# Weighing the values for two 64-query blocks at a time, left and right column halves of the array in turn

## The reference

```python
# layer 0: 16 heads of 8, values shared by 4 heads; window of 64 keys back
logits = masked_attn * gene_fitness[..., None] + (1.0 - mask) * -10000000000.0
attn_w = softmax(logits, axis=-1)
out = einsum('bhts,bhsd->bhtd', attn_w, v_full)        # then out @ w_o + b_o
# layer 1: 16 heads of 8, windows of 64 that overlap by half, blended
attn = softmax(einsum('bqd,bkd->bqk', qw, kw), axis=-1)
wo = einsum('bqk,bkd->bqd', attn, vw)                  # windows blended, then @ wproj + bproj
```

## Time and profile before

| | us |
|---|---|
| median of 2 runs | 1242.99 |
| lowest and highest run | 1239.91, 1246.08 |
| span of the profiled execution | 1243.5 |
| PE busy, weight loads busy | 793.3 (64%), 631.3 (51%) |
| DVE, ACT, POOL busy | 548.2, 305.2, 116.8 |

### The profile page before, as it was taken

How to read it: one execution, slowest core, us unless ns; L and a number is a source line. 1 busy time by engine, 2 the same in 40 slices (tenths; PEclk the granted TensorE clock), 3 DMA queues, 4 the chain that set the end, 5 groups by cost and what they waited for, 6 DMA issues and landing times.

```text
span 1243.5 us, 17236 instructions
## 1 busy us (share of the span) xinstructions
PE 793.3 (64%) x6608; PEld 631.3 (51%) x6608; DVE 548.2 (44%) x1386; ACT 305.2 (25%) x584; POOL 116.8 (9%) x139
## 2 busy tenths in 40 slices
PE   0623589658865886589074468756966795678055
PEld 0623367527652765277063347644855584467033
DVE  0261730573057205720266454557354656455232
ACT  0202431243124322431110123212213221231023
POOL 4140000000000000000522200000000000000500
PEclk9999765676567656755555675567557655855577
DMA  6004000400040004000100320041013002200101
GB/s 186 0 28 117 27 6 1 109 26 4 0 110 25 4 0 110 25 4 0 34 1 15 100 56 6 1 110 30 0 44 92 4 0 63 72 4 0 34 1 34
DMA packets 69458, 46.05 MB, mean 37 GB/s; under 512 B 13368, under 2 KB 60986, under 8 KB 69434
## 3 DMA queue, kind: packets, MB, share of 16 engines
q1 hardware_dynamic: 66970, 39.97, 11.6%
q0 software_dynamic: 2464, 5.77, 1.5%
HBM read 37.85 MB, written 7.86 MB: 37 GB/s over the span
## 4 chain that ended last, share of the span: by engine, by line
PE 48%; DVE 24%; ACT 8%; issue 6%; POOL 6%; SPq 4%; DMA 4%; POOLq 0%; DVEq 0%; ACTq 0%; another core or an unknown queue 0%
PE ps_turn L799 18%; PE ps_score L702 4%; DVE gm L570 3%; DVE tsum L568 3%; DVE gm L574 3%; PE ps_turn L689 3%; DMA b2r<-in_L_b2e 3%; PE ps_score L774 3%; PE ps_score L710 3%; POOL sorted_x L1049 2%; POOL moe L1058 2%; PE ps_score L778 2%; DVE v L515 2%; ACT qT L854 2%; PE ps_proj L809 2%
## 5 line engine op out<-in xcount | busy, mean ns | idle before, releaser
L799 PE MATMUL ps_turn<-v,pT 128*64 128x9 f32 (+1 forms) x2048 | 220.6, 276 | 6.7 <-ACT pT L890 4.4
L799 PEld LDWEIGHTS ps_turn<-v,pT 128*64 128x64 f32 x2048 | 214.4, 221 | 12.0 <-issue 8.1
L702 PE MATMUL ps_score<-xgT,w 128*128 128x128 f32 x384 | 88.4, 402 | 39.2 <-ACT xgT L833 39.2
L702 PEld LDWEIGHTS ps_score<-xgT,w 128*128 128x128 f32 x384 | 75.6, 293 | 54.6 <-ACT xgT L833 54.6
L456 POOL TENSOR_TENSOR ys<-ys,b2r 128x128 f32<-128x128 f32 x48 | 24.7, 515 | 823.0 <-ACT ys L844 823.0
L890 ACT ACTIVATE pT<-ps_score 128x1024 f32<-128x1024 f32 x64 | 64.7, 1023 | 136.9 <-PE ps_score L778 136.8
L699 PE MATMUL ps_score<-ident,xg 128*128 128x128 f32 x48 | 19.7, 411 | 96.6 <-DMA b2r<-in_L_b2e 64.7
L836 ACT ACTIVATE hT<-ps_score,b1s 128x128 f32<-128x128 f32 x192 | 54.7, 368 | 87.6 <-PE ps_score L702 87.6
L635 DVE RECIPROCAL wtot<-ps_turn 128x16 f32<-128x16 f32 x16 | 4.1, 257 | 161.9 <-PE ps_turn L799 161.9
L710 PE MATMUL ps_score<-w,hT 128*128 128x128 f32 x384 | 72.6, 364 | 0.0
L710 PEld LDWEIGHTS ps_score<-w,hT 128*128 128x128 f32 x384 | 71.5, 284 | 0.0
(11 more groups left out here) (215 smaller groups left out, 1331.6 us busy)
## 6 DMA issues: line engine op xcount, KB each, us to landing
w<-in_L_w1e SPq DMA_DIRECT2D x48, 256.0 KB, 2.8
w<-in_L_w2e SPq DMA_DIRECT2D x48, 256.0 KB, 3.0
xg<-sorted_x SPq DMA_DIRECT2D x48, 64.0 KB, 1.9
b2r<-in_L_b2e SPq DMA_DIRECT2D x48, 64.0 KB, 3.2
sorted_y<-ys SPq DMA_DIRECT2D x48, 64.0 KB, 1.6
sorted_x<-moe POOLq DMA_DIRECT2D x2, 768.0 KB, 7.3
out<-x SPq DMA_DIRECT2D x4, 256.0 KB, 2.3
b1s<-in_L_b1e SPq DMA_DIRECT2D x48, 2.0 KB, 2.6
```

The lines of the kernel that those rows point to most:

```text
L702: ins = te.matmul(ps_score[:, k, c * P:(c + 1) * P], w1[:, j % WS, c * P:(c + 1) * P], xgT[:, k, :], start=True, stop=True)
L799: ins = te.matmul(o, w_, r, start=True, stop=True)
```

## The change

`weigh` takes a tile of two blocks instead of one block; inside the loop over heads it issues the matmul of the even block and then that of the odd one, so that consecutive loads go to the left and the right 64 columns in turn. `s_pv` is raised once per tile. `probs` are issued two at a time, ahead of the `weigh` of the tile before. `pT` has four buffers; `th` is now the last two of them. ACT's order of work is the same; exp of block u waits for `weigh` of tile u // 2 - 2 from u = 4 on.

```diff
--- before.py
+++ after.py
@@ -139,8 +139,8 @@
         qT = sb("qT", [P, 8, T], BF16)
         kT = sb("kT", [P, 8, 64 + T + 64], BF16)
         v = sb("v", [P, NU, H * 36])
-        th = sb("th", [P, 2, 1024])
-        pT = sb("pT", [P, 2, 1024])
+        pT = sb("pT", [P, 4, 1024])
+        th = pT[:, 2:4, :]
         gm = sb("gm", [P, NT, H * 4])
         tsum = sb("tsum", [P, NT, H])
         inv = sb("inv", [P, NT, H])
@@ -629,7 +629,7 @@
                         keep_odd(2 * NT + t, qT[:, :, t * P:(t + 1) * P])
 
                     for t in range(NT):
-                        dv.wait_ge(s_pv, 2 * t + 2)
+                        dv.wait_ge(s_pv, t + 1)
                         if L == 0:
                             o = ps_turn[:, 0, 0:H * 9].rearrange("p (h e) -> p h e", e=9)
                             st(nc.vector.reciprocal(wtot[:, :], o[:, :, 8]))
@@ -781,22 +781,23 @@
                                                 start=m is None, stop=True, skip_group_check=True)
                         ins.then_inc(s_st, 1)
 
-                    def weigh(u):
-
-                        te.wait_ge(s_p, u + 1)
-                        t, blk = u // 2, u % 2
-                        if blk == 0 and t >= 1:
+                    def weigh(t):
+
+                        te.wait_ge(s_p, 2 * t + 2)
+                        if t >= 1:
                             te.wait_ge((s_hd if L == 0 else s_osb), t)
                         for h in range(H):
                             hf, par, j = h // 8, h // 4 % 2, h % 4
-                            w_ = pT[:, u % 2, par * 512 + (4 * hf + j) * 64:par * 512 + (4 * hf + j) * 64 + 64]
-                            if L == 0:
-                                o = ps_turn[64 * blk:64 * blk + 64, 0, 9 * h:9 * h + 9]
-                                r = v[:, u, 9 * (h // 4):9 * (h // 4) + 9]
-                            else:
-                                o = ps_turn[64 * blk:64 * blk + 64, hf, 36 * (h % 8):36 * (h % 8) + 36]
-                                r = v[:, u, 36 * h:36 * h + 36]
-                            ins = te.matmul(o, w_, r, start=True, stop=True)
+                            for blk in range(2):
+                                u = 2 * t + blk
+                                w_ = pT[:, u % 4, par * 512 + (4 * hf + j) * 64:par * 512 + (4 * hf + j) * 64 + 64]
+                                if L == 0:
+                                    o = ps_turn[64 * blk:64 * blk + 64, 0, 9 * h:9 * h + 9]
+                                    r = v[:, u, 9 * (h // 4):9 * (h // 4) + 9]
+                                else:
+                                    o = ps_turn[64 * blk:64 * blk + 64, hf, 36 * (h % 8):36 * (h % 8) + 36]
+                                    r = v[:, u, 36 * h:36 * h + 36]
+                                ins = te.matmul(o, w_, r, start=True, stop=True)
                         ins.then_inc(s_pv, 1)
 
                     def project(t):
@@ -810,14 +811,16 @@
                         te.matmul(ps_proj[:, 1, 0:D], ones[0:1, :], W[f"L{L}_bo"][:, :], start=False, stop=True).then_inc(s_op, 1)
 
                     probs(0)
-                    for u in range(NU):
-                        if u + 1 < NU:
-                            probs(u + 1)
-                        if u == 0:
+                    probs(1)
+                    for t in range(NT):
+                        if t + 1 < NT:
+                            probs(2 * t + 2)
+                            probs(2 * t + 3)
+                        if t == 0:
                             te.wait_ge(s_v, 2)
-                        weigh(u)
-                        if u % 2 == 1 and u >= 3:
-                            project(u // 2 - 1)
+                        weigh(t)
+                        if t >= 1:
+                            project(t - 1)
                     project(NT - 1)
 
 
@@ -885,9 +888,9 @@
 
                     for u in range(NU):
                         ac.wait_ge(s_st, u + 1)
-                        if u - 1 > 0:
-                            ac.wait_ge(s_pv, u - 1)
-                        nc.scalar.activation(pT[:, u % 2, :], ps_score[:, u % 2, :], ACT.Exp).then_inc(s_p, 1)
+                        if u >= 4:
+                            ac.wait_ge(s_pv, u // 2 - 1)
+                        nc.scalar.activation(pT[:, u % 4, :], ps_score[:, u % 2, :], ACT.Exp).then_inc(s_p, 1)
                         if u % 2 == 0 and u >= 4:
                             finish(u // 2 - 2)
                     finish(NT - 2)
@@ -907,7 +910,7 @@
             s_out_ = sem("m_out")
             hx = xnT[:, 0:2 * NT * D].rearrange("p (h n) -> p h n", h=2)
             hxT = xlT[:, 0:2 * T].rearrange("p (h n) -> p h n", h=2)
-            hidden = [b[:, :, :].rearrange("p a (b n) -> p (a b) n", n=T) for b in (th, pT)]
+            hidden = [b.rearrange("p a (b n) -> p (a b) n", n=T) for b in (th, pT[:, 0:2, :])]
 
             def vec(dv):
                 st = Steps(dv, dve_chain)
```

## The result

| | before | after |
|---|---|---|
| median of the runs, us | 1242.99 | 1132.76 |
| lowest and highest, us | 1239.91, 1246.08 | 1132.62, 1132.89 |
| span of the profiled execution, us | 1243.5 | 1131.0 |
| PE busy, weight loads busy, us | 793.3, 631.3 | 652.2, 510.8 |

The ratio is 0.912, with a 95% interval of 0.906 to 0.918. I had forecast 1158 us with a range from 1140 to 1174: the direction was right, the time lies 7 us under the range. The change took 110 us where I had counted on 85.

The account below looks back on a forecast made before the run. PE's 64-column f32 weight loads for L799, 18% of 1243.5 us, were taken to set the pace on the path. Savings of 46 us in layer 0 and 40 in layer 1 gave 1157.5, forecast 1158 us, range 1140 to 1174.

Parts of the forecast that it names:

- The two halves run beside one another: In `weigh`, left and right column halves both load at full pace: 64 matmuls in 3.5 us; chance 0.78.
- The rival's 6.93 us: Halves share the load path, so `weigh` of a tile costs 6.93 us and the kernel 1262 us; chance 0.08.
- The bound of 3.9 us for a limit of issue: In `weigh`, if 30 ns each is an issue limit, 128 loads and matmuls take 3.9 us; 11 us more, 1169.
- The new waits: PE waits for exps behind `finish`: 1.66 us before `weigh(3)`; before `probs(7)` 0.15 us in layer 0, 1.12 in layer 1.
- the walk: Weighing stage summed step by step on PE: 38.1 us cold in layer 0, 38.9 against 48.9 in layer 1.
- the new one starts some 2 us later, about when the clock falls: First `weigh` in three layer 0 stages gets little high clock; 11.4 us saved in each of the three.
- a cold stage: Layer 0 stage wholly at granted clock 0.5: 49.91 us before, 38.1 after, 11.8 less.
- the 86 of my sum: Saving over the eight weighing stages: 46 us in layer 0 and 40 in layer 1, from 386.98 to 301 us.
- The sign that I had named: The forecast counts as wrong if the granted clock of the stages leaves 0.50 to 0.57.
- the clock comes up: Denser matmuls lift the grant in `weigh`, 1.94 instead of 3.5 us; in a third to half, 1135 to 1145; chance 0.10.
- the argument against it: Against a higher clock: all of layer 1 stays at 0.50 with PE busy 41.95 of 48.9 us.

## Why the prediction was right in its mechanism and short in its size

**The two halves run beside one another: right, shown.** The pace is 3.49 us for 64 loads, 3.5 was forecast; alternation undone gives 6.50 back. (The rival's 6.93 us is 64 x 107 ns = 6.85 with the start.) The bound of 3.9 us for a limit of issue did not bind either: at the high clock 128 loads and matmuls went out in 1.95 us, 15 ns each. The rule of the Trainium skill's TensorE: Matmul & The Clock Gate, Part 3, that a load overlaps a running matmul only when row groups differ, does not hold for column halves here; that of its TensorEngine Tiling (Array Packing), Tiling Modes, does.

**The new waits: right.** 1.66 us before `weigh(3)` was worked out from ACT's order, 1.68 idle was measured, and moving the exps ahead took it away. In the last stage of layer 1 every step of the walk came within 0.4 us of its place, and the four stages gave 41.7 us, where 40 was forecast.

**The failed step: "the new one starts some 2 us later, about when the clock falls".** I took from the kernel before, where the grant fell at the end of the first `weigh`, that it would fall at the same time after; for the fourth stage, which had run at 0.5 throughout, I walked a cold stage. In the new kernel the clock stayed up for 10.9 to 12.5 us in all four. Up to the start of `probs(6)`, six `probs`, two `weigh` and a `project` cost 6 x 1.51 + 2 x 3.5 + 2.29 = 18.35 us at the low clock; the first stage took 180.91 - 169.67 = 11.24, 7.1 us less. From there to the end the walk has 19.78 us and the trace 19.46. So of 38.1 - 30.7 = 7.4 us the stretch at the high clock has 7.1. The four stages of layer 0 gave 68.7 us instead of 46: 22.7 of the 26.5 us between the 112.5 that the profiled span lost and the 86 of my sum. The sign that I had named came too: the granted clock of the layer 0 stages left 0.50 to 0.57. That the alternation is what keeps the clock up is shown by the two kernels that have the same stage with another order in `weigh`: in stages that began at 1.0 it fell after 6.1 to 7.4 us instead of 10.9 to 12.5, and in stages that began at 0.5 it fell 7.3 us in instead of 14.2.

**Why I gave this case 0.10.** I had it as a rival, "the clock comes up", at 1135 to 1145 us for a third to a half of the `weigh`s, and half of those of layer 0, a quarter of all, did run at the high clock. I priced `weigh` alone; but six `probs` of 0.87 instead of 1.51 us and a `project` gained in the same stretch, more than half of the 7.1 us. And the argument against it, layer 1 at 0.50 throughout, came from the layer where six of eight `probs` have no mask. There it held in three stages of four. The kernel without masks shows that layer 0 loses its high clock without them; that they are the whole difference between the layers is not shown, since three of the layer 1 stages also began 3 us after the grant had fallen, and in the kernel with the projects later it rose in layer 1 before the second of the two masks there. The earlier trace rows had shown layer 0 above 0.50 before.

**What stays open:** by what exactly the grant is decided. Shown is that it rose after `probs` with their masks on end, fell inside the first tile's `weigh` when that did not alternate at each matmul, fell at the start without the masks, and stayed up in layer 1 when `probs` stood in place of a wait. No run separates these from one another. Nor does the code of the stage alone decide how a stage begins: the fourth of layer 0 began at 0.5 in the kernel before and at 1.0 in the changed one, with the same code ahead of it.

## What to carry to other kernels

Where matmuls have few moving columns (9 and 36 here, with f32 weights), the weight load sets the pace, and loads of 64 columns into alternating halves of the array run two at a time: order the instructions so that the halves change at each one. Look for a place in the old trace where the new pattern already occurs once by accident, as the switch between blocks 6 and 7 did. And when a change makes TensorE denser, walk the stage at both clock levels, since the denser stretch may keep the high one, as layer 0 did here, and every matmul in it gains, also those that were not touched; then look at what the other engines' order in the code makes wait.

## What the runs showed of the hardware that I had not expected

- Taking work out of PE's queue made a stage slower: 32.38 us without the masks at a granted clock of 0.52, 30.70 us with them at 0.68. Adding eight dummy matmuls a batch in PE's idle time of layer 1 went with a faster kernel, 1089.4 against 1101.3 us.
- In two kernels whose layer 0 stages began at 0.5, the grant went to 1.0 after 3.9 us of masked `probs` (first stage of each). It then lasted 10.2 us where a `weigh` of 64 loads took 1.95 us, and 3.4 us where it took 2.53.
- With a change of half at every eighth load, 64 loads took 4.10 us, against 3.49 with a change at each and 6.50 with a single one: 0.40 us a change at 1.2 GHz, by my estimate about four matmuls.
